# One matrix product of a mixture-of-experts layer changed from split operands to plain fp32, with two transposed tiles moved ahead of a shared product

## What is computed

```
xf = layernorm(x).reshape(-1, 512)                      # 2048 tokens
gates = softmax(xf @ gate_w + gate_b)                   # 16 experts
topv, topi = top_k(gates, 2)
h  = gelu(einsum('nd,edh->neh', xf, ew1) + eb1)         # routed: 512 -> 128
eo = einsum('neh,ehd->ned', h, ew2) + eb2               # routed: 128 -> 512
routed = sum of the token's two experts, weighted by topv
hs = gelu(einsum('nd,sdh->snh', xf, sw1) + sb1)         # shared: 2 experts, 512 -> 2048
shared = einsum('snh,shd->nd', hs, sw2) + sum(sb2)      # 2048 -> 512
x = x + shared + routed
```

## Time and profile before

| | us |
|---|---|
| median of 3 runs (lowest, highest) | 921.85 (920.21, 922.37) |
| the profiled execution, its own time | 922.2 |
| its span, first to last instruction | 920.6 |
| TensorE busy in the span | 849.9 (92%) |
| VectorE, ScalarE, GpSimd busy | 647.8, 485.3, 179.5 |

### The profile page before, as it was taken

How to read it: one execution, slowest core, us unless ns; L and a number is a source line. 1 busy time by engine, 2 the same in 40 slices (tenths; PEclk the granted TensorE clock), 3 DMA queues, 4 the chain that set the end, 5 groups by cost and what they waited for, 6 DMA issues and landing times.

```text
span 920.6 us, 14811 instructions
## 1 busy us (share of the span) xinstructions
PE 849.9 (92%) x4018; PEld 695.8 (76%) x4018; DVE 647.8 (70%) x1345; ACT 485.3 (53%) x859; POOL 179.5 (19%) x223
## 2 busy tenths in 40 slices
PE   0198999999999999999999999999999899999997
PEld 0166878888788888887888888878888777777885
DVE  7985899856577778565777785645775777773774
ACT  5433866445366553453666534435553566775541
POOL 2000000012100000121000001210212666653660
PEclk9999999999999999999999999999999999999999
DMA  9144434458453333582533335655794466667885
GB/s 220 49 144 138 116 115 115 118 117 178 69 161 92 97 109 95 125 172 66 160 96 108 96 103 103 87 188 161 152 232 120 141 209 211 213 192 261 290 252 169
DMA packets 125855, 134.40 MB, mean 146 GB/s; under 512 B 10256, under 2 KB 87616, under 8 KB 125276
## 3 DMA queue, kind: packets, MB, share of 16 engines
q1 hardware_dynamic: 116844, 108.47, 44.5%
q0 software_dynamic: 8784, 25.11, 9.2%
q10 hardware_dynamic: 160, 0.02, 0.0%
HBM read 110.58 MB, written 22.98 MB: 145 GB/s over the span
## 4 chain that ended last, share of the span: by engine, by line
PE 91%; DVE 3%; issue 2%; DMA 2%; ACT 1%; SPq 1%; POOLq 0%; POOL 0%; DVEq 0%; ACTq 0%
PE up L561 13%; PE up L563 12%; PE up L562 12%; PE acc L604 12%; PE acc L609 12%; PE acc L606 12%; PE up L761 4%; PE up L763 2%; PE acc L561 2%; PE up L665 1%; PE acc L563 1%; PE acc L562 1%; PE misc L748 1%; PE up L748 1%; PE acc L674 1%
## 5 line engine op out<-in xcount | busy, mean ns | idle before, releaser
L561 PE MATMUL up<-xs,w1hi 128*128 128x512 f32 (+1 forms) x512 | 200.1, 391 | 5.3 <-ACT xs L896 4.6
L562 PE MATMUL up<-xs,w1hi 128*128 128x512 f32 (+1 forms) x512 | 196.5, 384 | 0.0
L563 PE MATMUL up<-xs,w1lo 128*128 128x512 f32 (+1 forms) x512 | 196.5, 384 | 0.0
L604 PE MATMUL acc<-w2hi,hhi 128*128 128x512 f32 x490 | 190.8, 389 | 1.3 <-issue 1.3
L606 PE MATMUL acc<-w2lo,hhi 128*128 128x512 f32 x490 | 190.7, 389 | 0.0
L834 ACT ACTIVATE hhi<-up,b_col 128x512 fp32r<-128x512 f32 (+1 forms) x128 | 86.8, 678 | 150.1 <-PE up L563 125.3
L1053 DVE TENSOR_TENSOR hlo<-hf,hhi 128x512 fp32r<-128x512 f32 (+1 forms) x128 | 86.0, 672 | 88.8 <-ACT hf L837 56.3
L609 PE MATMUL acc<-w2hi,hlo 128*128 128x512 f32 x490 | 131.7, 389 | 0.0
L561 PEld LDWEIGHTS up<-xs,w1hi 128*128 128x128 f32 x512 | 96.2, 188 | 24.9 <-ACT xs L896 5.2
L563 PEld LDWEIGHTS up<-xs,w1lo 128*128 128x128 f32 x512 | 96.2, 188 | 19.4
L562 PEld LDWEIGHTS up<-xs,w1hi 128*128 128x128 f32 x512 | 96.3, 188 | 18.3 <-issue 0.2
(11 more groups left out here) (243 smaller groups left out, 1135.8 us busy)
## 6 DMA issues: line engine op xcount, KB each, us to landing
w_raw<-in_L_ffn_sw SPq DMA_DIRECT2D x270, 256.0 KB, 3.1
expert_rows<-ysb SPq DMA_DIRECT2D x47, 256.0 KB, 2.5
vin<-in_ctx SPq DMA_DIRECT2D x16, 256.0 KB, 8.4
xn_rows<-kn POOLq DMA_DIRECT2D x16, 256.0 KB, 8.0
e2raw<-in_L_ffn_ew SPq DMA_DIRECT2D x16, 256.0 KB, 5.1
ew_sb<-in_L_ffn_ew SPq DMA_DIRECT2D x16, 256.0 KB, 7.0
X<-in_x SPq DMA_DIRECT2D x12, 256.0 KB, 9.9
out<-X SPq DMA_DIRECT2D x12, 256.0 KB, 4.6
```

What stands on the lines that cost most here:

```text
L561: nc.tensor.matmul(o, lhs[0], rhs[0], start=start, stop=False)
L562: nc.tensor.matmul(o, lhs[0], rhs[1], start=False, stop=False)
L563: return nc.tensor.matmul(o, lhs[1], rhs[0], start=False, stop=stop)
L604: nc.tensor.matmul(acc[t][:], hh, w2hi[:, slot], start=first and (q > 0 or t >= HT) or again, stop=False)
```

## The change

The routed up product is made in plain fp32. The weights are copied by GpSimd unrounded (`take_w1` in place of `cast_w1`), VectorE copies the turned tokens unrounded (`routed_x`), and TensorE makes four fp32 matmuls of 128 columns per slot. ScalarE's token copy, VectorE's two lo subtractions and the sum go away; ScalarE's Gelu reads the up product from PSUM. On GpSimd gather(s) now stands behind take_w1(s-1). T(0) and T(1) are issued in `step(113)`, ahead of the down product of chunk 113 (`first_tiles`), and take_w1(0) is made before that product is done; waits for semaphores that this makes needless are left out, and TensorE no longer waits for the last row copy before the shared up products of chunks 114 and 115.

```diff
@@ -125,14 +126,14 @@
         w1_raw = sb("w1_raw", [P, RING, KC, P], where=ring_mem)
         ring_mem.close()
         routed_mem = ExitStack()
-        xgp = sb("xgp", [P, 2, KC, 2, P], f32r, routed_mem)
-        xghi, xglo = xgp[:, :, :, 0], xgp[:, :, :, 1]
-        e1hi = sb("e1hi", [P, 3, KC, P], f32r, routed_mem)
-        e1lo = sb("e1lo", [P, 3, KC, P], f32r, routed_mem)
+        e1_first = sb("e1_first", [P, KC, P], where=routed_mem)
+        xgT = sb("xgT", [P, XB, KC, P], where=routed_mem)
+        e1_next = sb("e1_next", [P, 2, KC, P], where=routed_mem)
+        e1 = [e1_first, e1_next[:, 0], e1_next[:, 1]]
         rf = sb("rf", [P, RB, P], where=routed_mem)
         rhi = sb("rhi", [P, RB, P], f32r, routed_mem)
+        rlo = sb("rlo", [P, RB, P], f32r, routed_mem)
         ysb = sb("ysb", [P, YB, D], where=routed_mem)
-        rlo = sb("rlo", [P, 2, P], f32r, routed_mem)
         routed_mem.close()
         sb("rings", [P, 9 * RING * D])
 
@@ -579,6 +579,22 @@
                 pe.wait_ge(xhi_ok, TB * (q + 1))
                 pe.wait_ge(xlo_ok, TB * (q + 1))
 
+            def routed_T(s):
+                i = s % 2
+                pe.wait_ge(g_in[s % 4], 16 * (s // 4 + 1))
+                need(pe, rxc, s - 1)
+                for k in range(KC):
+                    last = nc.tensor.transpose(t_bank[i][:, P * k:P * k + P], xg[:, s % 4, P * k:P * k + P],
+                                               ident[:])
+                last.then_inc(rT, 1)
+
+            def first_tiles():
+                pe.wait_ge(tvec.sem, tvec.at(0))
+                pe.wait_ge(h_hi, HOLD - 2)
+                pe.wait_ge(h_full, HOLD - 2)
+                routed_T(0)
+                routed_T(1)
+
             class step:
                 engine = pe
 
@@ -591,6 +607,8 @@
                         block_ready(ahead // CH)
                     if not isinstance(c, int) or ahead < HOLD or c >= HOLD and ahead < NCH:
                         up_product(c + 2, ahead, ahead // CH)
+                    if isinstance(c, int) and c == HOLD - 1:
+                        first_tiles()
                     need(pe, w2_hi, c + 1)
                     need(pe, w2_lo, c + 1)
                     need(pe, h_hi, c + 1)
@@ -739,49 +757,29 @@
                     pe.wait_ge(rt.sem, rt.at(TB * (q + 1) - 1, "rank"))
                     gate_product(q + 1)
 
-            def routed_T(s):
-                i = s % 2
-                pe.wait_ge(g_in[s % 4], 16 * (s // 4 + 1))
-                need(pe, rxh, s - 1)
-                need(pe, rxl, s - 1)
+            def routed_up(s):
+                pe.wait_ge(r1, s + 1)
+                pe.wait_ge(rxc, s + 1)
+                need(pe, rhh, s - 1)
+                need(pe, rff, s - 1)
                 for k in range(KC):
-                    last = nc.tensor.transpose(t_bank[i][:, P * k:P * k + P], xg[:, s % 4, P * k:P * k + P],
-                                               ident[:])
-                last.then_inc(rT, 1)
-
-            def routed_up(s):
-                i = s % 2
-                pe.wait_ge(rxh, s + 1)
-                pe.wait_ge(rxl, s + 1)
-                pe.wait_ge(r1hi, s + 1)
-                pe.wait_ge(r1lo, s + 1)
-                need(pe, rsm, s - 1)
-                for k in range(KC):
-                    both = xgp[:, i, k].rearrange("p a n -> p (a n)")
-                    nc.tensor.matmul(r_bank[i][:, 0:2 * P], e1hi[:, s % 3, k], both, start=k == 0, stop=False)
-                for k in range(KC):
-                    last = nc.tensor.matmul(r_bank[i][:, 0:P], e1lo[:, s % 3, k], xghi[:, i, k], start=False,
-                                            stop=k == KC - 1)
+                    last = nc.tensor.matmul(r_bank[s % 2][:, 0:P], e1[s % 3][:, k], xgT[:, s % XB, k],
+                                            start=k == 0, stop=k == KC - 1)
                 last.then_inc(rup, 1)
 
             def routed_down(s):
-                i, h = s % 2, s % RB
-                e = pe.value_load(rvT[0:1, s:s + 1], min_val=0, max_val=E - 1)
+                e, h = pe.value_load(rvT[0:1, s:s + 1], min_val=0, max_val=E - 1), s % RB
                 pe.wait_ge(rhh, s + 1)
                 pe.wait_ge(rhl, s + 1)
                 need(pe, rye, s - 1)
-                splits(y_bank[i][:], (rhi[:, h], rlo[:, i]), (e2hi[:, e], e2lo[:, e]), True, True).then_inc(ry, 1)
-
-
-            pe.wait_ge(tvec.sem, tvec.at(0))
+                splits(y_bank[s % 2][:], (rhi[:, h], rlo[:, h]), (e2hi[:, e], e2lo[:, e]), True, True).then_inc(ry, 1)
+
+
             pe.wait_ge(h_hi, HOLD)
             pe.wait_ge(h_full, HOLD)
-            routed_T(0)
-            routed_T(1)
             routed_up(0)
             routed_T(2)
             routed_up(1)
-
             pe.wait_ge(r2hi, E)
             pe.wait_ge(r2lo, E)
             pe.wait_ge(acc_free, TB * (NQ - 1) + len(y_bank))
@@ -792,10 +790,12 @@
                     routed_up(s + 2)
                 routed_down(s)
 
-            pe.wait_ge(rsm, SLOT_TILES)
-            pe.wait_ge(rye, SLOT_TILES)
+            pe.wait_ge(rxc, SLOT_TILES)
+            pe.wait_ge(rhh, SLOT_TILES)
+            pe.wait_ge(rff, SLOT_TILES)
             up_product(HOLD, HOLD, NQ - 1)
             up_product(HOLD + 1, HOLD + 1, NQ - 1)
+            pe.wait_ge(rye, SLOT_TILES)
             last_chunks(step, until=NCH - 2)
             for c in (NCH - 2, NCH - 1):
                 pe.wait_ge(w2_hi, c + 1)
@@ -984,29 +984,16 @@
 
 
             act.wait_ge(tvec.sem, tvec.at(0))
-            act.wait_ge(ew_in, 16 * E)
             act.wait_ge(down_done, HOLD)
-            act.wait_ge(h_lo, HOLD)
-            act.wait_ge(w2_lo, HOLD)
-            act.wait_ge(w2_hi, HOLD)
-            act.wait_ge(h_full, HOLD)
-
-            def routed_x(s):
-                i = s % 2
-                act.wait_ge(rT, s + 1)
-                need(act, rup, s - 1)
-                nc.scalar.copy(xghi[:, i], t_bank[i][:].rearrange("p (k n) -> p k n", k=KC)).then_inc(rxh, 1)
 
             def routed_h(s):
                 i = s % RB
                 b = bslot[:, s:s + 1]
-                act.wait_ge(tvec.sem, tvec.at(0))
-                act.wait_ge(rsm, s + 1)
+                act.wait_ge(rup, s + 1)
                 need(act, ry, s - RB + 1)
-                nc.scalar.activation(rhi[:, i], rf[:, i], ACT.Gelu, bias=b).then_inc(rhh, 1)
-                act.wait_ge(tvec.sem, tvec.at(0))
-                act.wait_ge(rhh, s + 1)
-                nc.scalar.activation(rf[:, i], rf[:, i], ACT.Gelu, bias=b).then_inc(rff, 1)
+                need(act, rhl, s - RB + 1)
+                nc.scalar.activation(rhi[:, i], r_bank[s % 2][:, 0:P], ACT.Gelu, bias=b).then_inc(rhh, 1)
+                nc.scalar.activation(rf[:, i], r_bank[s % 2][:, 0:P], ACT.Gelu, bias=b).then_inc(rff, 1)
 
             def routed_y(s):
                 n = s % YB
@@ -1014,18 +1001,12 @@
                 need(act, yst[n], 16 * (s // YB))
                 nc.scalar.copy(ysb[:, n], y_bank[s % 2][:]).then_inc(rye, 1)
 
-            routed_x(0)
-            routed_x(1)
             routed_h(0)
-            routed_x(2)
+            routed_h(1)
             for s in range(SLOT_TILES):
-                if s + 1 < SLOT_TILES:
-                    routed_h(s + 1)
-                if s + 3 < SLOT_TILES:
-                    routed_x(s + 3)
-                if s:
-                    routed_y(s - 1)
-            routed_y(SLOT_TILES - 1)
+                if s + 2 < SLOT_TILES:
+                    routed_h(s + 2)
+                routed_y(s)
 
             act.wait_ge(ry, SLOT_TILES)
             for n in range(YB):
@@ -1527,63 +1508,32 @@
                 schedule(q, step, head, half, mid, tile, late, final, extra)
 
 
-            after(tvec, 0, None)
-            dve.wait_ge(ew_in, 16 * E)
-            dve.wait_ge(down_done, HOLD)
-            dve.wait_ge(w1_lo, HOLD)
-            dve.wait_ge(w2_lo, HOLD)
             dve.wait_ge(h_lo, HOLD)
 
-
-            def routed_w1(s):
-                i = s % 3
-                e = dve.value_load(rvT[0:1, s:s + 1], min_val=0, max_val=E - 1)
-                dve.wait_ge(r1hi, s + 1)
-                need(dve, rup, s - 2)
-                V.tensor_tensor(e1lo[:, i], ew1_sb[:, e], f(e1hi[:, i]), ALU.subtract).then_inc(r1lo, 1)
-
             def routed_x(s):
-                i = s % 2
-                dve.wait_ge(rxh, s + 1)
-                need(dve, rup, s - 1)
-                V.tensor_tensor(xglo[:, i], t_bank[i][:].rearrange("p (k n) -> p k n", k=KC), f(xghi[:, i]),
-                                ALU.subtract).then_inc(rxl, 1)
-
-            def routed_sum(s):
-                i = s % 2
-                dve.wait_ge(rup, s + 1)
-                need(dve, rhl, s - RB + 1)
-                V.tensor_reduce(rf[:, s % RB], r_bank[i][:, 0:2 * P].rearrange("p (a n) -> p n a", a=2), AX.X, ALU.add)\
-                    .then_inc(rsm, 1)
+                dve.wait_ge(rT, s + 1)
```

(43 more changed lines are left out.)

## The result

The changed kernel took 912.46 us in the median of 4 runs (908.2 to 914.43), the kernel before beside it 922.11: ratio 0.9891 (95% interval 0.9851 to 0.9930). The forecast was 905.4 us, 1.8% less; it is 1.1% less. That is inside the stated range of 896 to 914, but outside the 900.5 to 911 that the forecast's own branch covered. The profiled execution is the slowest of the four, 914.43 us with a span of 912.8.

What follows compares the result with a forecast made beforehand. The routed stage was taken as nearly TensorE-bound, held by a VectorE-ScalarE circle of 2.51 us a slot. Savings of 10.6 (slots), 4.4 (start) and 1.5 us (end), 16.5 together, gave 905.4 us, range 896 to 914.

Steps and rivals of the forecast that it cites:

- the forecast's own branch: Routed stage: gather chain slightly above TensorE's pace, the kernel at 900.5 to 911 us; chance 0.55.
- The plain fp32 up product: Routed slots on TensorE: eight matmuls 0.11 us apart, 0.88 us a slot in place of 0.94.
- L734's spacing: Upper bound for the routed up product: plain fp32 matmuls 0.21 us apart, 1.68 us a slot.
- rival 3: Routed up product at 0.21 us spacing: slots of 2.88 us, the kernel slower at 932 us; chance 0.04.
- the circle: Routed slots: VectorE and ScalarE wait on each other, 2.51 us a slot, 0.37 of it TensorE's wait; the edit cuts it.
- The copy on VectorE and the shared port: Routed slots: VectorE's new copy reads PSUM, so doesn't lock GpSimd out; if it did, 10 us worse.
- The chain through GpSimd: Routed stage: up product, weight copy, gather, landing, transposes, up product three slots on; three slots need 2.82 us plus landing.
- Rival 1: Routed stage: TensorE sets the pace throughout, landings near 3.3 us, slots of 2.08 us, kernel at 898 us; chance 0.25.
- the landing L: Routed gathers: landing time of 3.2 to 5.1 us, median 3.5, and 4.4 in the median from 795 us on.
- the first stall: Start of the routed stage: T(4) waits for its gather behind up(0), 1.4 to 1.5 us.
- Rival 2: Routed stage: crowded gathers land in 4.4 us throughout, 2.41 us a slot, kernel at 913.7 us; chance 0.12.

Runs made afterwards that it cites:

- e1: The changed kernel with gather(4) and gather(5) issued behind take_w1(0) and gather(s+3) behind take_w1(s): 893.63 us, ratio 0.9704 to the kernel before.
- e7: e4 without the weight cast's wait for ScalarE's token copy, its wait for the up product kept: 921.86 us against 921.49 for the kernel before, ratio 1.0002.
- e2: The changed kernel storing only 8 of each slot's 128 result rows: 44 slots take 97.93 us instead of 109.25; its whole time says nothing.
- e3: The changed kernel with the slot table's empty places filled with different token numbers instead of token 0: 906.3 us, ratio 0.9837 to the kernel before.
- e4: The kernel before with the changed kernel's GpSimd order, gather(s) behind cast_w1(s-1), three casts first: 943.58 us, ratio 1.0229.
- e8: The kernel before with the slot table's empty places spread over different tokens: 921.24 us against 921.49, ratio 0.9999.

## Why the prediction came out as it did

- **The plain fp32 up product** was forecast at 0.88 us, where the old one took 0.94. It is 0.81 (763.09 to 763.90), the slot 2.03 instead of 2.08. L734's spacing is out, and with it rival 3, the slower one.
- **VectorE, ScalarE, the circle**: right. It is cut, and TensorE waits for neither of them from 717 to 827 us.
- **The copy on VectorE and the shared port**: right. GpSimd was not held up: a gather's issue takes 0.98 us (0.97 before) and its weight copy 0.61, as before, while VectorE copies from PSUM.
- **The chain through GpSimd**: right in mechanism; e1 and e7 show it from both sides. Its constant is 2.5 to 2.6 us, where 2.82 was forecast: the 0.3 us put between landing and first transpose are at most 0.1. Over 42 slots that error alone would have made the forecast 3 to 4 us too slow, and it hid a part of the next one. Rival 1's traffic would rise by a fifth (2.51 to 2.08 us a slot) and not by the sixth that the prediction gives; no other number hangs on it.
- **Mis-sized, first: the landing L.** The step put it at 3.3 for 8 slots, 3.75 for 28 and 4.9 for 8, taken from a kernel that issued gathers at one fixed place in a slot of 2.51. It measures 4.7 in the median and up to 6.4, and 4.9 to 5.5 for the last six gathers; 42 slots took 101.2 us where 94.4 were forecast (98.6 less two at 2.08). This is the step that failed, a term too small: 6.8 of the 9.2 us missing. e2 shows that most of the excess over 2.03 goes with the stores beside the gathers, e3 that a part goes with the repeated row. Why the gathers land 1.2 us later than in the kernel before (3.5), with the same stores and only 7% more GB/s, stays open. The late order alone doesn't do it: in e4, where gathers are issued as late but a slot takes 3.05 us, the 38 that TensorE's matmuls wait for reach their transposes 3.6 us after issue in the median. The faster pace is left, or that gathers come in bunches after each wait, which the uneven gaps make likely; neither was tried by itself.
- **Mis-sized, second: the first stall.** Forecast 1.4 us over 2.08. It is 2.8 over 2.03, and the slot behind takes 3.29 instead of 2.03, for the clock, full until 720.5, is at half from 721 to 724 us, after 2.19 us of idle time: 4.0 together. GpSimd makes take_w1(1), (2) and (3) ahead of gather(4) (714.53 to 716.52); I had counted one of the three, and the gather starts 1.0 us later than by my sum. It lands in 3.9 us where I had 3.4, and the half clock, in the transposes and the slot behind, I had put at nothing.
- **Rival 1** (898 us, TensorE sets the pace) is what e1 makes of the kernel (893.6 us, with slots of 2.03 and no first stall), by the order on GpSimd and not by faster landings. **Rival 2** (landings of 4.4 throughout, 913.7 us) is nearest to what was measured, in its mechanism too; I gave it 0.12 and should have given it more. That it comes within 1.3 us is in part luck, for its landing is 0.3 too short and its constant 0.3 too long. The forecast kept its range only by the width left for this rival.

## What to carry to other kernels

When the circle between two engines is cut, look for the next chain through a transfer: its length divided by the number of slots it spans is a lower bound for the slot. Count the spans in the program list, with every wait in front of the transfer's issue (e4 shows what one overlooked wait costs), and leave the transfer behind nothing but the release of its own buffer. A transfer's landing time taken from a slower schedule may be too short for the faster one; here 3.5 us became 4.7.

## What the runs showed of the hardware

A plain fp32 product of 128 columns shows as two matmuls, 0.112 us apart (eight in 1.06 us with a tail of 0.275), so that the up product in plain fp32 takes 0.81 us where the split one took 0.94. Whether the weight loads set this spacing or the columns do isn't told, since both were worked out at 0.11 us.

Reading one row of memory over and over lengthens a gather: spreading the unused places took 5.7 us off a stage paced by gathers (e3), and nothing off one that isn't (e8).

VectorE's low part of h (L1523, two SBUF inputs) takes 282 ns in the median, but up to 737 ns in e1:

```profile
L1523 DVE TENSOR_TENSOR rlo<-rf,rhi x41: 281/282/737, 718.5 to 799.7; 128x128 fp32r<-128x128 f32 x41
```

The longest one lies beside one of GpSimd's weight copies, and ends 0.15 us after it:

```profile
718.42 0.63 POOL L1689 COPY e_next<-ew_sb 128x512 f32 x1
718.46 0.74 DVE L1523 TENSOR_TENSOR rlo<-rf,rhi 128x128 fp32r<-128x128 f32 x1
```

One slot on, where it starts 0.29 us after a weight copy, it takes 0.48 us; beside a gather's issue (757.07 us, for one) it takes 0.28. This agrees with SBUF — State Buffer, SBUF: two separate sides, of the Trainium skill, by which a VectorE operation with two SBUF inputs and a GpSimd one that reads SBUF exclude each other.
